# Two attention layers on one core: bias lines of a head group written in one transfer from a mirrored grid, and the normalising product moved from VectorE to GpSimd

## The chip, the cores and the metric

One Trainium2 chip, of which the kernel uses a single core. The metric is the device time in microseconds (us). The kernel before was timed three times: median 1791.99 us, lowest 1791.25, highest 1793.11. The time after comes from the same measurement.

## The reference

The input is x of shape (8, 256, 32, 32): 8 batch elements, 256 channels, 1024 positions. Two layers follow each other. The shapes of the weights are left out.

```python
# layer 0
xn = (x - mean) / jnp.sqrt(var + EPS) * gamma          # mean and variance over the channels
q, k, v = jnp.split(einsum('oc,bcn->bon', w_qkv, xn), 3, axis=1)   # 8 heads of 32
sim = einsum('bhdi,bhdj->bhij', q, k) * scale
bias = _cpb_bias(32, w0, b0, w1, b1, w2, b2)           # a small network of (yi - yj, xi - xj), per head
out = einsum('bhij,bhdj->bhdi', softmax(sim + bias), v)
x = einsum('oc,bcn->bon', w_out, out) + x
# layer 1
f, g, h = Wf x + bf, Wg x + bg, Wh x + bh              # f, g of 32 channels, h of 256
attn = softmax(einsum('bno,bom->bnm', f, g), axis=2)
return gamma * einsum('bci,bij->bcj', h, attn) + x
```

The bias depends only on the difference of two positions, so a table of 63 x 63 values for each head holds all of it.

## The kernel before, in words

The 8 heads are two groups g of HG = 4, one for each half of 256 channels. For each batch element b the kernel goes through four phases: the rows of group 0, the columns of group 0, the rows of group 1, the columns of group 1, each of 32 tiles of 128 x 1024 scores.

- In a **rows** phase (tile m) TensorE computes the scores of 128 queries against all keys (L587, L588), VectorE adds the bias and takes the maximum (L1015), and ScalarE exponentiates and sums (L829). This gives each query its shift.
- In a **columns** phase (tile n) TensorE computes scores again, transposed and with the shift folded in (L608), VectorE adds the bias (L1029), ScalarE exponentiates (L846), and TensorE multiplies by v (L635).

All engines run their programs in order and meet at semaphores. Everything else is placed beside these tiles by four tables written by hand, `side_0`, `column_0`, `side_1` and `column_1`: an entry `(3, "norm", 0)` of `column_0` stands behind tile n = 3 of the columns of group 0. In this way the normalisation and the q and k of element b+1 (kinds "mean", "centre", "square", "var", "rstd", "norm", "k0", "q0") and layer 1 of element b-1 are done beside element b. Of the normalisation, "centre" (L873) subtracts the mean on VectorE, "rstd" (L716, L712) leaves 1/std in `o[:, 1]`, and "norm" (L879) multiplies the two halves of `xn` by it, each 128 x 1024 floats, on VectorE. TensorE's "k0", first needed behind n = 14, and all later users of `xn` wait for it through the semaphore `normed`.

q and k change their layout by a trip through DRAM. They are split into a high and a low part in the buffer `st` (ScalarE writes the high part, VectorE the low one, kinds "high_..." and "low_..."), `q_out` and `k_out` (L298) write `st` to `q_parts` and `k_parts`, and `q_in` (L311, 6 transfers) and `k_in` (L325, 3 transfers) load `q_stack` and `k_stack`. `st` is one buffer for both, so the next high part waits until the transfer before it has been stored.

The bias is brought into place once, at the start. A small network on TensorE, ScalarE and VectorE computes the table, SP stores it to DRAM (L367, L368), and then for each group g and each column x = 0 ... 31 one transfer `lines_out` (L330) copies 252 runs of 32 floats (4 heads x 63 rows) from the table to `bias_lines` in DRAM: for group 0 sixteen are issued by SP and sixteen by ScalarE, for group 1 all 32 by SP. SP waits until a group is stored, and then `bias_in` (L362) loads it to `bias_lines_sb` by 16 transfers of 240 KB. Group 0's first rows tile needs the first head of group 0; group 1's rows phase needs group 1. Behind `bias_in(1)` in SP's program stand `q_out` and `q_in` of group 1 and the load of x for element 1.

ScalarE at the start: it computes 1/std, waits for the table, issues its sixteen `lines_out`, and only then does it handle `high_k0`, `k_out`, `high_q0`, `q_out`, `k_in`, `q_in` of element 0, after which the first rows tile can start.

As the stored table runs with rising difference, the keys or queries of one side are read backwards: the moving operand of L587 and L588 is `back(keys, ...)`, that of L608 is `q_stack[..., ::-1]`.

Of the kernel before, what the change touches and what calls it, by code (L numbers as in the profile page):

```python
# [25 lines left out]
def two_layer_attention(nc, x, mlp_in, rel_in, wqkv_in, gamma_in, ident_in, wout_in, wh_in, wfg_in, bfg_in,  # L26
# [23 lines left out]
    with ExitStack() as ctx:  # L50
# [82 lines left out]
        lines_stored = sem("lines_stored")  # L133
        late_lines_stored = sem("late_lines_stored")
# [27 lines left out]
        VECTOR = dict(centered=KC, normed=KC, lo_ready=2 * (NHALF + 1), a_max=G * HG * NT, scaled=G * NHALF,  # L162
# [6 lines left out]
        for kind in (TENSOR, VECTOR, SCALAR):  # L169
            for name, n in kind.items():  # L170
                counted(name, n)
# [31 lines left out]
        column_0 = [(1, "rstd", 1), (3, "norm", 0), (9, "norm", 1)]  # L203
# [69 lines left out]
        def row_tile(m):  # L273


            r, rest = divmod(m, HM)
            h, t = divmod(rest, NT // NHALF)
            return r, h, (NHALF - 1 - r) * (NT // NHALF) + t
# [49 lines left out]
        def lines_out(eng, g, x, done):  # L328
            src = table_dram.ap().rearrange("h (a w) -> h a w", w=DX)[g * HG:(g + 1) * HG, :, W - 1 - x:2 * W - 1 - x]
            eng.dma_start(lines_dram.ap()[g, x], src).then_inc(done, 16)  # L330

# [3 lines left out]
        def _(sp):  # L335
# [6 lines left out]
            def shift_to_stack(b, g, r):  # L342

                need(sp, "rows_ready", b, g * NHALF + r + 1)
                for part in range(2):
                    sp.dma_start(q_stack[KS + part:KS + part + 1, g, NHALF - 1 - r].bitcast(F32)
                                 .rearrange("p h (t n) -> p (h t) n", n=P),
                                 shift_rows[part * HM:(part + 1) * HM, r, :].bitcast(F32)).then_inc(rows_loaded, 16)
# [10 lines left out]
            def bias_in(g):  # L359
                for h in range(HG):  # L360
                    for yl in range(ROWS):
                        sp.dma_start(bias_lines[yl * W:(yl + 1) * W, g * HG + h],  # L362
                                     lines_dram.ap()[g, :, h, ROWS - 1 - yl:ROWS - 1 - yl + NA]
# [7 lines left out]
            for x in range(0, W, 2):  # L371
                lines_out(sp, 0, x, lines_stored)
            sp.wait_ge(lines_stored, 16 * W)
            bias_in(0)
            for x in range(W):
                lines_out(sp, 1, x, late_lines_stored)
            sp.wait_ge(late_lines_stored, 16 * W)
            bias_in(1)
# [30 lines left out]
        def _(pe):  # L409
# [167 lines left out]
            def row_tiles(b, g, first, m):  # L577
# [9 lines left out]
                pe.matmul(psum[:, bank, :], lhsT, back(keys, 0, HALF, N), start=True, stop=True)  # L587
                pe.matmul(psum[:, bank + 1, :], lhsT, back(keys, HALF, HALF, N), start=True,  # L588
# [8 lines left out]
            def columns_phase(b, g, first, last):  # L597


                for q in range(TG + PV_LAG):  # L600
                    if q < TG:
                        for n in range(q * HP, (q + 1) * HP):
# [4 lines left out]
                            for i in range(2):  # L607
                                mm = pe.matmul(psum[:, bank + i, :], k_stack[:, g, 2 * j + i, t * P:(t + 1) * P],  # L608
                                               q_stack[:, g, NHALF - 1 - half, 2 * j + i, ::-1],
# [81 lines left out]
        def _(act):  # L691
# [87 lines left out]
            def output(b, g, half, last):  # L779
# [83 lines left out]

        @block.vector
        def _(dve):
# [3 lines left out]
            def do(kind, arg, b, g, first, last, tail=False):  # L869
# [127 lines left out]
            for k in range(KC):  # L997
                do("norm", k, 0, 1, True, False)
# [4 lines left out]
            def element(b, first, last):  # L1003
                for g in range(G):
                    for m in range(A_TILES):
                        r, h, t = row_tile(m)
                        a0 = (H - ROWS - ROWS * t) * W
# [12 lines left out]
                    for n in range(SN):  # L1020
                        half, t, j = column_tile(n)
                        a0 = (half * (H // NHALF) - ROWS * t + H - ROWS) * W
# [35 lines left out]
def relative_grid(side):  # L1058

    d = np.arange(1 - side, side, dtype=np.float32)  # L1060
# [61 lines left out]
```

## Time and profile before

| | before |
|---|---|
| median of 3 runs | 1791.99 us |
| the profiled execution, its own time | 1792.51 us |
| its span, first to last instruction | 1790.7 us |
| TensorE, busy | 1590.5 us (89%) |
| VectorE, busy | 1478.0 us (83%) |
| ScalarE, busy | 1382.0 us (77%) |
| GpSimd, busy | 7.1 us |
| DMA moved | 122.71 MB, 58121 packets, 22292 of them under 512 B |
| mean granted TensorE clock | 0.936 |

The span is what the trace covers, the execution's own time has 1.8 us around it. Busy time of TensorE is not time at its peak, since its matmuls overlap, and a mean over the span hides stages: the page's row of 40 slices shows TensorE at 6, 2 and 6 tenths in its first three slices of 44.8 us, and at 8 or 9 nearly everywhere after.

### The profile page before, as it was taken

How to read it: one execution, taken by the hardware profiler on the slowest of the kernel's cores; microseconds unless marked ns; L12 is line 12 of the kernel's file. 1: busy time of each engine (PE TensorE's matmuls, PEld its weight loads, DVE VectorE, ACT ScalarE, POOL GpSimd, SP SyncE). 2: the span in 40 equal slices, each digit the busy share in tenths (PEclk: the TensorE clock that was granted, in tenths of full speed). 3: DMA queues.
4: the chain of work that ended last, by engine and by line, in shares of the span. 5: the costliest groups of instructions: out<-in, count | busy, mean ns of one | idle time of the engine just before them, and what ended most of it. 6: DMA issues, size and time to landing. Idle time of an engine off the chain costs nothing.

```text
span 1790.7 us, 18676 instructions
## 1 busy us (share of the span) xinstructions
PE 1590.5 (89%) x5976; PEld 754.6 (42%) x5976; DVE 1478.0 (83%) x2168; ACT 1382.0 (77%) x2033; POOL 7.1 (0%) x5
## 2 busy tenths in 40 slices
PE   6268899899998999889998999989998999989988
PEld 2033334345353444435453443535444453535424
DVE  3157988898988988898888989898888989899853
ACT  2066889778887878878787888888798788889743
POOL 1000000000000000000000000000000000000000
PEclk8577869999999999999999999999999999999999
DMA  3972204320350203501152203502034102500100
GB/s 87 221 173 69 59 1 130 95 59 1 89 157 4 59 1 107 141 24 36 46 159 45 59 1 107 142 1 60 25 117 108 51 10 80 141 4 0 37 12 23
DMA packets 58121, 122.71 MB, mean 69 GB/s; under 512 B 22292, under 2 KB 23828, under 8 KB 58024
## 3 DMA queue, kind: packets, MB, share of 16 engines
q1 hardware_dynamic: 50952, 114.85, 23.3%
q10 hardware_dynamic: 7072, 6.68, 1.5%
q8 instruction: 47, 0.77, 0.2%
q14 instruction: 50, 0.41, 0.1%
HBM read 78.92 MB, written 44.13 MB: 69 GB/s over the span
## 4 chain that ended last, share of the span: by engine, by line
PE 49%; DVE 24%; issue 18%; SPq 3%; ACT 3%; DMA 2%; ACTq 1%; DVEq 0%
DVE biased L1015 13%; PE psum L533 9%; PE psum L608 9%; PE psum L635 8%; PE psum L587 5%; DVE biased L1029 5%; PE psum L413 5%; PE psum L588 4%; PE psum L456 3%; SPq L330 2%; PE psum L490 2%; PE psum L466 1%; ACT biased L829 1%; DMA xn<-in_x_dram 1%; ACT probs L846 1%
## 5 line engine op out<-in xcount | busy, mean ns | idle before, releaser
L1015 DVE CUSTOM_DVE_ANT_0 biased<-psum,bias_lines_sb 128x1024 f32<-128x1024 f32 x512 | 617.3, 1222 | 157.5 <-PE psum L588 150.1
L829 ACT ACTIVATE biased<-biased,nmax 128x1024 f32<-128x1024 f32 x512 | 587.2, 1147 | 140.5 <-DVE nmax L1015 136.1
L846 ACT ACTIVATE probs<-biased 128x1024 f32<-128x1024 f32 x512 | 536.5, 1056 | 127.9 <-DVE biased L1029 107.5
L1029 DVE TENSOR_TENSOR biased<-psum,bias_lines_sb 128x1024 f32<-128x1024 f32 x512 | 598.0, 1220 | 44.7 <-PE psum L608 34.2
L608 PE MATMUL psum<-q_stack,k_stack 98*128 98x512 f32 x1024 | 393.5, 492 | 39.3 <-DVE nmax L1015 16.2
L587 PE MATMUL psum<-k_stack,q_stack 96*128 96x512 f32 x512 | 330.2, 645 | 92.7 <-DVE nmax L1015 48.5
L608 PEld LDWEIGHTS psum<-q_stack,k_stack 98*128 98x128 f32 x1024 | 179.0, 201 | 328.2 <-issue 152.5
L635 PE MATMUL psum<-probs,vT 128*32 128x512 f32 x2048 | 283.5, 623 | 6.1 <-DVE st L896 3.9
L587 PEld LDWEIGHTS psum<-k_stack,q_stack 96*128 96x128 f32 x512 | 99.9, 195 | 277.1 <-DVE nmax L1015 176.4
L588 PE MATMUL psum<-k_stack,q_stack 96*128 96x512 f32 x512 | 211.8, 414 | 0.0
L533 PE MATMUL psum<-probs 128*128 128x512 f32 x384 | 186.6, 592 | 0.0
L588 PEld LDWEIGHTS psum<-k_stack,q_stack 96*128 96x128 f32 x512 | 102.7, 201 | 49.9 <-issue 46.4
L456 PE MATMUL psum<-xn,wqkvT 128*128 128x512 f32 x128 | 79.8, 718 | 26.1 <-DVE st L896 7.8
L829 ACT ACTIVATION_READ_ACCUMULATOR biased<-biased,nmax 128x1 f32 x512 | 96.2, 188 | 0.0
L533 PEld LDWEIGHTS psum<-probs 128*128 128x128 f32 x384 | 72.6, 189 | 46.4 <-issue 36.1
L635 PEld LDWEIGHTS psum<-probs,vT 128*32 128x32 f32 x2048 | 42.5, 109 | 101.2 <-issue 74.3
L767 ACT ACTIVATE probs<-probs,nmax 128x1024 f32<-128x1024 f32 x48 | 54.9, 1144 | 16.3 <-DVE probs L953 15.6
L413 PE MATMUL psum<-xn,wqkvT 128*128 128x512 f32 x128 | 66.4, 600 | 0.0
L466 PE MATMUL psum<-wqkvT,xn 128*128 128x256 f32 x256 | 65.7, 378 | 0.0
L502 PE MATMUL psum<-whT,x 128*128 128x256 f32 x256 | 65.5, 380 | 0.0
L478 PE MATMUL psum<-o,woutT 128*128 128x512 f32 x128 | 64.4, 593 | 0.8 <-ACT o L788 0.8
L533 PE MATMUL psum<-o,probs 128*128 128x512 f32 x128 | 64.8, 592 | 0.0
(78 smaller groups left out, 1091.0 us busy)
## 6 DMA issues: line engine op xcount, KB each, us to landing
q_stack<-q_parts SPq DMA_DIRECT2D x90, 256.0 KB, 5.5
k_stack<-k_parts SPq DMA_DIRECT2D x45, 512.0 KB, 7.4
q_parts<-st SPq DMA_DIRECT2D x15, 1024.0 KB, 3.9
k_parts<-st SPq DMA_DIRECT2D x15, 1024.0 KB, 4.2
xn<-in_x_dram SPq DMA_DIRECT2D x8, 1024.0 KB, 8.9
x<-in_x_dram SPq DMA_DIRECT2D x8, 1024.0 KB, 9.5
out_dram<-x SPq DMA_DIRECT2D x8, 1024.0 KB, 4.1
bias_lines_sb<-bias_lines SPq DMA_DIRECT2D x32, 240.0 KB, 8.0
```

The lines of the kernel that those rows point to most:

```text
L413: mm = pe.matmul(psum[0:rows, bank + half, :], lhsT(k), src[:, k, half * HALF:(half + 1) * HALF], start=(k == 0), stop=(k == KC - 1))
L456: mm = pe.matmul(psum[:, bank, :], wqkvT[:, k, t * C:t * C + P], xn[:, k, half * HALF:(half + 1) * HALF], start=(k == 0), stop=(k == KC - 1))
L466: mm = pe.matmul(psum[:, 4 + arg % 2, 0:C], xn[:, k, arg * P:(arg + 1) * P], wqkvT[:, k, 2 * C:3 * C], start=(k == 0), stop=(k == KC - 1))
L533: mm = pe.matmul(psum[:, 4 + 2 * c + half, :], hs[:, t % HS, c * P:(c + 1) * P], attn1[t % 3][:, half * HALF:(half + 1) * HALF], start=(t ...
L587: pe.matmul(psum[:, bank, :], lhsT, back(keys, 0, HALF, N), start=True, stop=True)
L588: pe.matmul(psum[:, bank + 1, :], lhsT, back(keys, HALF, HALF, N), start=True, stop=True).then_inc(SEMS["a_mm"], 1)
L608: mm = pe.matmul(psum[:, bank + i, :], k_stack[:, g, 2 * j + i, t * P:(t + 1) * P], q_stack[:, g, NHALF - 1 - half, 2 * j + i, ::-1], star ...
L635: mm = pe.matmul(psum[h * HD:(h + 1) * HD, 4 + half, :], vT[:, t, (g * HG + h) * HD:(g * HG + h + 1) * HD], probs[:, ((q - PV_LAG) * HP + ...
L829: nc.scalar.activation(biased[:, m % BIASED, :], biased[:, m % BIASED, :], ACT.Exp, scale=-1.0, bias=nmax[:, m:m + 1], accum_out=rowsum[:, ...
L846: nc.scalar.activation(probs[:, n % P_SLOTS], biased[:, n % BIASED, :] .rearrange("p (i n) -> p i n", i=2), ACT.Exp).then_inc(SEMS["probs_ ...
L1015: nc.vector.tensor_tensor_reduce(biased[:, m % BIASED, :], pair(bank_of(g, first, ("rows", m))), bias_lines[:, g * HG + h, a0:a0 + N], -1. ...
L1029: nc.vector.tensor_tensor(biased[:, n % BIASED, :].rearrange("p (i n) -> p i n", i=2), psum[:, bank:bank + 2, :], bias_lines[:, g * HG + 2 ...
```

## The change

There are two edits that are independent of each other.

**The lines.** The grid of differences is built with falling instead of rising differences (`np.arange(side - 1, -side, -1)`), so the table is mirrored in both directions. The line of column x now starts at x in each table row, and the 32 columns of a group are one access pattern of overlapping runs: 32 x 252 x 32 floats with steps 1, 63, 1. Each group is one transfer, both are issued by SP, one behind the other and each with its own semaphore. ScalarE issues none. The two `bias_in` follow behind both. The rest follows the mirror: where a tile's bias starts (`a0`), the order of the two halves of the queries, keys and queries read forwards, and the output `o` written backwards.

**The product.** "norm" goes out of VectorE's program and out of `column_0`. GpSimd multiplies both halves of `xn` by 1/std, as soon as "centre" and "rstd" are done.

```diff
-        column_0 = [(1, "rstd", 1), (3, "norm", 0), (9, "norm", 1)]
+        column_0 = [(1, "rstd", 1)]
...
-            for x in range(0, W, 2):
-                lines_out(sp, 0, x, lines_stored)
-            sp.wait_ge(lines_stored, 16 * W)
-            bias_in(0)
-            for x in range(W):
-                lines_out(sp, 1, x, late_lines_stored)
-            sp.wait_ge(late_lines_stored, 16 * W)
-            bias_in(1)
+            for g in range(G):
+                src = bass.AP(tensor=table_dram.ap().tensor, offset=g * HG * DY * DX,
+                              ap=[[1, W], [DX, HG * DY], [1, W]])
+                sp.dma_start(lines_dram.ap()[g].rearrange("x h a w -> x (h a) w"), src).then_inc(lines_stored[g], 16)
+            for g in range(G):
+                sp.wait_ge(lines_stored[g], 16)
+                bias_in(g)
...
-                pe.matmul(psum[:, bank, :], lhsT, back(keys, 0, HALF, N), start=True, stop=True)
-                pe.matmul(psum[:, bank + 1, :], lhsT, back(keys, HALF, HALF, N), start=True,
+                pe.matmul(psum[:, bank, :], lhsT, keys[:, 0:HALF], start=True, stop=True)
+                pe.matmul(psum[:, bank + 1, :], lhsT, keys[:, HALF:N], start=True,
...
-                                               q_stack[:, g, NHALF - 1 - half, 2 * j + i, ::-1],
+                                               q_stack[:, g, half, 2 * j + i, :],
...
-                nc.scalar.copy(o[:, g, half * HALF:(half + 1) * HALF],
-                               psum[:, 4 + half, :]).then_inc(SEMS["o_ready"], 1)
+                nc.scalar.copy(back(o[:, g, :], half * HALF, HALF, N), psum[:, 4 + half, :]).then_inc(SEMS["o_ready"], 1)
...
-            act.wait_ge(table_stored, 32)
-            for x in range(1, W, 2):
-                lines_out(nc.scalar, 0, x, lines_stored)
...
+            def normalise(b, k):
+                need(pool, "centered", b, KC)
+                need(pool, "rstd_ready", b, 2)
+                nc.gpsimd.tensor_tensor(xn[:, k, :], xn[:, k, :], rstd, ALU.mult).then_inc(SEMS["normed"], 1)
+
+            for b in range(B):
+                for k in range(KC):
+                    normalise(b, k)
...
-                elif kind == "norm":
-                    if arg == 0:
-                        need(dve, "rstd_ready", b, 2)
-                        need(dve, "centered", b, KC)
-                    nc.vector.tensor_tensor(xn[:, arg, :], xn[:, arg, :], rstd, ALU.mult).then_inc(SEMS["normed"], 1)
...
-    d = np.arange(1 - side, side, dtype=np.float32)
+    d = np.arange(side - 1, -side, -1, dtype=np.float32)
```

SP's program at the start, before: `bias_table` is the stored table, `bias_lines` the lines in DRAM, `bias_lines_sb` those in SBUF.

```order
L367 DMA bias_table<-probs 8x2016 [waits table_ready]
L368 DMA bias_table<-probs 8x1953
L330 DMA bias_lines<-bias_table 252x32 [waits table_stored]
L330 DMA bias_lines<-bias_table 252x32 x15
L362 DMA bias_lines_sb<-bias_lines 32x1920 [waits lines_stored]
L362 DMA bias_lines_sb<-bias_lines 32x1920 x15
L330 DMA bias_lines<-bias_table 252x32 x32
L362 DMA bias_lines_sb<-bias_lines 32x1920 [waits late_lines_stored]
L362 DMA bias_lines_sb<-bias_lines 32x1920 x15
L298 DMA q_parts<-st 128x2x1024 [waits q_loaded,lo_ready]
```

The same stretch of SP's program now.

```order
L363 DMA bias_table<-probs 8x2016 [waits table_ready]
L364 DMA bias_table<-probs 8x1953
L370 DMA bias_lines<-bias_table 8064x1x32 [waits table_stored]
L370 DMA bias_lines<-bias_table 8064x1x32
L358 DMA bias_lines_sb<-bias_lines 32x1920 [waits lines_stored_0]
L358 DMA bias_lines_sb<-bias_lines 32x1920 x15
L358 DMA bias_lines_sb<-bias_lines 32x1920 [waits lines_stored_1]
L358 DMA bias_lines_sb<-bias_lines 32x1920 x15
L298 DMA q_parts<-st 128x2x1024 [waits q_loaded,lo_ready]
```

48 transfers of SP became two, and the 32 loads of the bias now stand behind each other with nothing but a semaphore between them.

VectorE's program in the columns phase of group 0, element 0, before: L1029 adds the bias to a tile, L923 to L935 are the shift.

```order
L1029 TENSOR_TENSOR biased<-psum,bias_lines_sb 128x1024 x4
L879 TENSOR_TENSOR xn<-xn,o 128x1024
L1029 TENSOR_TENSOR biased<-psum,bias_lines_sb 128x1024
L923 TENSOR_TENSOR invsum<-rowsum,invsum 128x16
L926 SCALAR_TENSOR_TENSOR lnsum<-invsum,lnsum 128x16
L929 TENSOR_TENSOR shift<-nmax,lnsum 128x16
L932 CAST shift_hi<-shift 128x16
L934 COPY shift_parts<-shift_hi 128x16
L935 TENSOR_TENSOR shift_parts<-shift,shift_hi 128x16
L1029 TENSOR_TENSOR biased<-psum,bias_lines_sb 128x1024 x5
L879 TENSOR_TENSOR xn<-xn,o 128x1024
L1029 TENSOR_TENSOR biased<-psum,bias_lines_sb 128x1024 x10
```

The same place now (the lines have other numbers: L1024 adds the bias, L920 to L932 are the shift).

```order
L1024 TENSOR_TENSOR biased<-psum,bias_lines_sb 128x1024 x5
L920 TENSOR_TENSOR invsum<-rowsum,invsum 128x16
L923 SCALAR_TENSOR_TENSOR lnsum<-invsum,lnsum 128x16
L926 TENSOR_TENSOR shift<-nmax,lnsum 128x16
L929 CAST shift_hi<-shift 128x16
L931 COPY shift_parts<-shift_hi 128x16
L932 TENSOR_TENSOR shift_parts<-shift,shift_hi 128x16
L1024 TENSOR_TENSOR biased<-psum,bias_lines_sb 128x1024 x15
```

The two products are gone from between the tiles. They are now 16 instructions on GpSimd, `xn<-xn,o 128x1024`, behind its fill of `k_stack`.

## Rows read from the trace of the kernel before

**Rows 1.** Timeline, the start: start us, us, engine, line, operation [idle before, releaser].
```profile
30.40 2.36 DVE L879 TENSOR_TENSOR xn<-xn,o 128x1024 f32<-128x1024 f32 x2 [0.56 <-ACT o L712]
32.73 7.84 SPq L330 DMA_DIRECT2D bias_lines<-bias_table  x10
32.91 6.54 PE L456 MATMUL psum<-xn,wqkvT 128*128 128x512 f32 x8 [3.83 <-DVE xn L879]
...
45.70 1.08 ACT L732 ACTIVATE st<-psum 128x512 fp32r<-128x512 f32 x2 [15.33 <-issue]
47.62 9.45 SPq L362 DMA_DIRECT2D bias_lines_sb<-bias_lines  x16
54.36 0.60 ACT L728 ACTIVATE st<-psum 128x512 fp32r<-128x512 f32 x1 [7.57 <-DMA k_parts<-st]
57.12 43.93 SPq L330 DMA_DIRECT2D bias_lines<-bias_table  x32
60.82 0.38 ACTq L298 DMA_DIRECT2D q_parts<-st  x1
86.38 0.77 PE L587 MATMUL psum<-k_stack,q_stack 96*128 96x512 f32 x1 [26.95 <-DMA q_stack<-q_parts]
102.76 7.81 SPq L362 DMA_DIRECT2D bias_lines_sb<-bias_lines  x16
102.95 1.22 DVE L882 SCALAR_TENSOR_TENSOR st<-psum,st 128x1024 fp32r<-128x1024 f32 x1
```

**Rows 2.** Windows: busy us of each engine, granted clock, DMA share, GB/s.
```profile
54.00:57.00 3.00, 1.17 (x2) 0.69 (x3) 0.69 (x1) 0.60 (x1) 0.00 (x0) 0.50 1.04 223
81.00:84.00 3.00, 0.00 (x0) 0.00 (x0) 0.00 (x0) 0.00 (x0) 0.00 (x0) 0.50 1.11 229
93.00:96.00 3.00, 3.00 (x12) 2.13 (x11) 1.23 (x2) 1.60 (x4) 0.00 (x0) 0.95 0.32 41
```

**Rows 3.** The chain that ended last, stretch 32 to 137 us: start us, us, what.
```profile
60.24 7.06 SPq L330
...
93.56 0.73 SPq L330
94.33 0.73 SPq L330
...
110.70 13.61 DMA q_parts<-st
127.11 9.13 DMA xn<-in_x_dram
136.29 2.07 PE psum L413 x2
```

**Rows 4.** DMA issues: engine, count, KB each, median us to landing.
```profile
q_parts<-st SPq DMA_DIRECT2D x15, 1024.0 KB, 3.9
bias_lines_sb<-bias_lines SPq DMA_DIRECT2D x32, 240.0 KB, 8.0
```

**Rows 5.** The chain around the first product, element 3's columns, group 0.
```profile
763.03 0.06 DVE xn L879
764.16 1.22 DVE biased L1029
```

**Rows 6.** The chain around the second product, elements 3 and 0.
```profile
174.94 1.00 issue
175.94 1.23 DVE biased L1029
...
773.16 0.67 PE psum L608 x2
773.83 0.86 PE psum L490 x2
```

**Rows 7.** Timeline: GpSimd's fill, and element 3's first use of the product.
```profile
0.73 6.92 POOL L862 MEMSET k_stack<- 2x8192 f32 x1 [0.29 <-POOLq L1109]
...
780.09 1.10 PE L456 MATMUL psum<-xn,wqkvT 128*128 128x512 f32 x2 [1.14 <-issue]
```

More of the change, by code:

```diff
@@ L132, in two_layer_attention @@
         table_stored = sem("table_stored")
-        lines_stored = sem("lines_stored")
-        late_lines_stored = sem("late_lines_stored")
+        lines_stored = [sem(f"lines_stored_{g}") for g in range(G)]
         consts_set = sem("consts_set")
@@ L161, in two_layer_attention @@
                       pv_mm=G * TG, proj_mm=KC * NHALF, fg_mm=3, h_mm=NT, s1_mm=NT, sa_mm=NT)
-        VECTOR = dict(centered=KC, normed=KC, lo_ready=2 * (NHALF + 1), a_max=G * HG * NT, scaled=G * NHALF,
+        POOL = dict(normed=KC)
+        VECTOR = dict(centered=KC, lo_ready=2 * (NHALF + 1), a_max=G * HG * NT, scaled=G * NHALF,
                       shifted=2 * G * NHALF, split_hi=G * NHALF,
@@ L168, in two_layer_attention @@
                       rows_ready=G * NHALF, probs_ready=G * TG * HP, o_ready=G * NHALF, fg_hi=3, e1_ready=NT, hs_ready=NT)
-        for kind in (TENSOR, VECTOR, SCALAR):
+        for kind in (TENSOR, VECTOR, SCALAR, POOL):
             for name, n in kind.items():
@@ L277, in row_tile @@
             h, t = divmod(rest, NT // NHALF)
-            return r, h, (NHALF - 1 - r) * (NT // NHALF) + t
+            return r, h, r * (NT // NHALF) + t
         def column_tile(n):
@@ L326, in k_in @@
                              k_dram.ap()[part].rearrange("h d n -> d h n")).then_inc(k_loaded, 16)
-        def lines_out(eng, g, x, done):
-            src = table_dram.ap().rearrange("h (a w) -> h a w", w=DX)[g * HG:(g + 1) * HG, :, W - 1 - x:2 * W - 1 - x]
-            eng.dma_start(lines_dram.ap()[g, x], src).then_inc(done, 16)
         block = ctx.enter_context(nc.Block())
@@ L345, in shift_to_stack @@
                 for part in range(2):
-                    sp.dma_start(q_stack[KS + part:KS + part + 1, g, NHALF - 1 - r].bitcast(F32)
+                    sp.dma_start(q_stack[KS + part:KS + part + 1, g, r].bitcast(F32)
                                  .rearrange("p h (t n) -> p (h t) n", n=P),
@@ L362, in bias_in @@
                         sp.dma_start(bias_lines[yl * W:(yl + 1) * W, g * HG + h],
-                                     lines_dram.ap()[g, :, h, ROWS - 1 - yl:ROWS - 1 - yl + NA]
+                                     lines_dram.ap()[g, :, h, yl:yl + NA]
                                      .rearrange("x a w -> x (a w)")).then_inc(lines_loaded[g * HG + h], 16)
@@ L862, in _ @@
             nc.gpsimd.memset(k_stack[KS:KS + 2].bitcast(F32), 1.0).then_inc(ones_set, 1)
+            pool.wait_ge(ones_set, 1)
+            def normalise(b, k):
[5 more added lines that the diff above has]
+                    normalise(b, k)
         @block.vector
@@ L996, in _ @@
                     do("centre", 0, 0, 1, True, False)
-            for k in range(KC):
-                do("norm", k, 0, 1, True, False)
             dve.wait_ge(consts_loaded, 16 * N_CONSTS)
@@ L1006, in element @@
                         r, h, t = row_tile(m)
-                        a0 = (H - ROWS - ROWS * t) * W
+                        a0 = ROWS * t * W
                         free = (("sum_ready", b, g * A_TILES + m - BIASED + 1) if m >= BIASED else
@@ L1021, in element @@
                         half, t, j = column_tile(n)
-                        a0 = (half * (H // NHALF) - ROWS * t + H - ROWS) * W
+                        a0 = (half * (H // NHALF) + ROWS * t) * W
                         need(dve, "s_mm", b, g * SN + n + 1)
```

## The prediction

> **What bounds the kernel now.** I read the timeline of the start first, because half of the change is there. The reader is to see three things in it [rows 1]. TensorE does not begin the first rows tile before 86.38 us, and waits 26.95 us for the load of `q_stack`. ScalarE could take the first half of k0 from TensorE soon after 36 us, but is at its own sixteen lines transfers and starts at 45.70. And the first VectorE instruction of element 0 that is not a rows tile, the low part of q, comes at 102.95, sixteen us after the first tile.
>
> Then the windows, for what the 16 DMA engines do meanwhile [rows 2]. Their share is 1.04 in 54 to 57 us, where the bias of group 0 is loaded at 223 GB/s, and 1.11 in 81 to 84: from about 48.5 to 86.3 us the transfers themselves set the time. In 93 to 96 the share is 0.32: there SP issues the lines of group 1 one by one, and the engines are mostly idle.
>
> The chain of waits shows that the start does not end at 86 us [rows 3]. SP gets to `q_out` of group 1 only at 110.70, since the sixteen loads of the bias stand before it; the store takes 13.61 us, and has 3.9 in the median of the later ones [rows 4]. The load of x follows (127.11, 9.13 us), and TensorE takes up the "mean" of element 1 at 136.29. From there on the engines set the pace, not the DMA.
>
> In the columns phases of group 0 the chain goes alternately over VectorE and TensorE. The first product lies on it: 763.03 to 764.16 is the product, and the next tile waits behind it [rows 5]. When VectorE reaches the second product of element 3, the chain is on TensorE (773.16, 773.83); in element 0, which has no layer 1 beside it, the second one is on the chain too (174.94, 1.00 us) [rows 6].
>
> **The product, part by part.** Sixteen instructions leave VectorE. Two are at the start and are treated below. Of the 14 others, the first of each of 7 elements is on the chain with 764.16 - 763.03 = 1.13 us [rows 5], 7 x 1.13 = 7.9. In element 0 the second adds 1.0, in the six others I take 0 (below: 0; above: 1.1 each, 6.6 in all, if VectorE were behind there; I take the end that the chain shows). TensorE has to be able to follow: it has waits for VectorE at this place that are about as long as the product, so I let all of it count. Together -8.9 us.
>
> On GpSimd the trace shows no such product. From below: the fill of 8192 floats a partition takes 6.92 us [rows 7], so 1024 floats cost 0.86 us for the writing alone; from above three such passes, two read and one written, 2.6 us. I take 2.6, for what reads as well as writes is nearer to it. Two of them end 5.2 us after 1/std. That is ready at about 763, and "k0" is first issued at 780.09 [rows 7], so 12 us cover it. If the cover were gone, it would cost what the products exceed 17 us by.
>
> What GpSimd does beside VectorE might slow VectorE. The trace has no pair of the two at work together on large tiles, so this price is open: none from below, and from above VectorE standing still for the 5.2 us of each of 7 elements, 36 us. I take 0, as the tiles of VectorE in this stretch read one operand from PSUM and one from SBUF.
>
> A rule of the Trainium skill bears on that (GPSIMD Engine Reference, sections 3.1 and 8): GpSimd needs 4497 ns for a product of 2048 floats a partition, about twice VectorE, and shares its SBUF interface with VectorE, which collides when the VectorE instruction has two SBUF inputs. By its figure one product here would be an estimated 2.2 us. By its condition the bias additions would not collide, and the six small instructions of the shift would. No row here shows either.
>
> **The lines.** What goes: the 64 single transfers, sixteen of them on ScalarE. What comes: two of SP, one behind the other. Work for the engines: 32 transfers of a group take, at the pace of SP, 94.33 - 93.56 = 0.77 us each [rows 3], at a share of 0.32 [rows 2], which makes 0.25 us of all sixteen engines; 64 of them are 15.7 us. Bounds for both groups together: 12 us from below, if fuller queues let the small packets follow each other more closely, and 49 us from above (64 x 0.77), if one queue cannot run faster than SP's single transfers did. I take 15.7, because that pace is SP's issue time, and the engines stood idle for two thirds of it.
>
> They begin at about 35 (table stored 32.7, 2.3 us until data moves) and end at about 50.7. Beside them the start of element 0 goes on: products on GpSimd end at 30.3 + 5.2 = 35.5 instead of 32.8, TensorE is 2.7 us later, and ScalarE takes k0 as it comes, so `k_out` is issued at about 43 instead of 47.7. But its data queue behind two large transfers of SP. I let them land when the lines are done, near 54, as before (54.36 [rows 1]). The 2.7 us of GpSimd and the 9 us of freed ScalarE are both hidden by that.
>
> Now the loads. Before, `q_stack` landed at 86.3 after 37.8 us of full engines, which carried the bias of group 0, both stores and both loads, and about 1.3 us of lines of group 1: 36.5 without them. Now SP issues the 16 loads of group 1 right behind those of group 0 (a group takes SP 9.45 us [rows 1]), so that they are in the queue before `q_out` is issued (60.82 before, about 59.5 now). They are 16 x 240 KB = 3.93 MB, at 229 GB/s [rows 2] 17.2 us. So the first tile starts at 50.7 + 36.5 + 17.2 = 104.4 instead of 86.4: +18.0.
>
> What this buys: behind the start there is no load of the bias any more. `q_out` of group 1 is issued when its low part is done, 102.95 + 1.22 = 104.2 on the old clock instead of 110.7 (-6.5), and lands in 3.9 us instead of 13.61 (-9.7) [rows 1, 3, 4]. Together -16.2. The load of x keeps its 9 us, as it still runs beside `q_in`. So "mean" of element 1 starts at 136.3 + 18.0 - 16.2 = 138.1, +1.8 us. A transfer that was to come early has only changed its place in a full queue.
>
> The Trainium skill says (DMA: Bandwidth & Descriptors, Rules for kernel authors) that many small transfers should be made one large one. Taken alone it would have the start of the tiles move forward by about the 9 us that ScalarE and SP save; by the windows above the queue is full right afterwards, and the saving does not reach the tiles.
>
> Reading and writing forwards or backwards I take as equal: the number of elements is the same, and no row shows both directions of one of these operations. That is an assumption, and the matmuls in the middle would show it.
>
> **Sum.** 1792.5 (the profiled execution) - 8.9 + 1.8 = 1785.4. The median of the runs is 0.5 lower, so 1785.
>
> **The rivals.**
> - *The transfers of q and k go first* (0.2). If the DMA engines serve ScalarE's queue in turn with or ahead of the long bias loads, only few of group 1's 17.2 us lie ahead of the first tile. It starts near 87, and the rest of the bias, then x, follow beside the tiles: "mean" near 122. That is -14 at the start, 1769 in all. For it: k0's store, issued beside the bias loads, was quick. Against it: q's store, issued at 60.82, took until 71.67.
> - *One queue is slow* (0.14). This is the other side. If the two large transfers move at the pace of SP's single ones, both need up to 49 us; each us above 15.7 delays the first tile by one, since ScalarE's k0 and the bias wait behind. From 15.7 + 7.1 + 3.6 = 26 us on the kernel is slower by more than 0.2%; at 36 us, halfway to the bound, it is 1785 + 20 = 1805. Against it: the share of 0.32.
> - *GpSimd slows VectorE, or TensorE does not follow* (0.2). Then the 8.9 us are lost in part or wholly; with 1.8 at the start, 1787 to 1794, with heavy collisions above 1800.
>
> **How the numbers follow.** My forecast has 0.46, with its own range 1780 to 1790. What a measurement can tell from no change is 0.2%, 3.6 us, so faster is below 1788.4 and slower above 1795.6. Faster: 0.36 of the forecast, 0.2 of the first rival, 0.03 of the third. Same: 0.1 of the forecast, 0.02 of the second, 0.1 of the third. Slower: 0.12 of the second and 0.07 of the third. The range 1767 to 1802 reaches to the first rival and some way into the second.
>
> **What would show it.** In the profile after: the two lines transfers end near 51 us; the share of the DMA engines is near 1 from there to the first tile, near 104; `q_parts` of group 1 lands in about 4 us; "mean" of element 1 starts near 138; the products take 2 to 2.6 us on GpSimd and the bias additions on VectorE keep 1.22. The forecast is wrong if the first tile starts before 95 or after 115, if the additions beside a product are longer, or if the length of an element in the middle does not fall by about 1.1 us.

## The result

The changed kernel takes 1802.78 us in the median (1801.11 to 1804.38, four runs), the kernel before 1792.55 beside it. The ratio is 1.0056 with a 95% interval of 1.0041 to 1.007: slower by 10 us, where 1785 was forecast. The time lies just outside the range. The two edits went in opposite directions: the start became shorter, where it was forecast 1.8 us longer, and each element that has a product beside its columns became longer.

| | before | after |
|---|---|---|
| profiled execution: span | 1790.7 us | 1799.3 us |
| TensorE / VectorE / ScalarE busy | 1590.5 / 1478.0 / 1382.0 us | 1588.5 / 1482.5 / 1382.2 us |
| GpSimd busy | 7.1 us | 44.6 us |
| mean granted TensorE clock | 0.936 | 0.934 |
| first rows tile starts | 86.38 us | 95.73 us |
| "mean" of element 1 starts | 136.29 us | 131.03 us |

VectorE has sixteen instructions less, 19.4 us of work, and is busy for 4.5 us more. That is the first thing to notice. The groups of instructions by line say where it went (busy us, mean ns of one, then idle time before them). First two rows of the shift before:

```profile
L926 DVE SCALAR_TENSOR_TENSOR lnsum<-invsum,lnsum 128x16 f32<-128x16 f32 x32 | 5.6, 174 | 1.1
L923 DVE TENSOR_TENSOR invsum<-rowsum,invsum 128x16 f32<-128x16 f32 x32 | 5.4, 170 | 0.0
```

The same after, with the product and the bias additions:

```profile
L1024 DVE TENSOR_TENSOR biased<-psum,bias_lines_sb 128x1024 f32<-128x1024 f32 x512 | 597.5, 1216 | 53.3 <-PE psum L603 39.8 <-ACT biased L820 7.7 <-ACT probs L837 2.9
L860 POOL TENSOR_TENSOR xn<-xn,o 128x1024 f32<-128x1024 f32 x16 | 37.5, 2366 | 1349.2 <-ACT o L707 1349.2
L923 DVE SCALAR_TENSOR_TENSOR lnsum<-invsum,lnsum 128x16 f32<-128x16 f32 x32 | 20.2, 632 | 1.1
L920 DVE TENSOR_TENSOR invsum<-rowsum,invsum 128x16 f32<-128x16 f32 x32 | 13.1, 409 | 0.0
```

Two instructions on 16 floats a partition cost 22.3 us more (20.2 - 5.6 + 13.1 - 5.4), while the 512 large additions have kept their 1.22 us. The timeline of element 3, at the place of [rows 5], shows the moment:

```profile
765.04 4.70 POOL L860 TENSOR_TENSOR xn<-xn,o 128x1024 f32<-128x1024 f32 x2 [203.61 <-ACT o L707]
...
766.17 1.30 DVE L920 TENSOR_TENSOR invsum<-rowsum,invsum 128x16 f32<-128x16 f32 x1
...
767.51 2.26 DVE L923 SCALAR_TENSOR_TENSOR lnsum<-invsum,lnsum 128x16 f32<-128x16 f32 x1
769.80 0.17 DVE L926 TENSOR_TENSOR shift<-nmax,lnsum 128x16 f32<-128x16 f32 x1
...
770.62 0.61 PE L567 MATMUL psum<-ident,shift_parts 128*32 128x128 f32 x2 [3.37 <-DVE shift_parts L932]
...
771.66 1.22 PE L603 MATMUL psum<-q_stack,k_stack 98*128 98x512 f32 x2 [0.43 <-DVE biased L1024]
...
772.82 1.93 PE L630 MATMUL psum<-probs,vT 128*32 128x512 f32 x8
```

GpSimd's two products run from 765.04 to 769.74. L920 starts inside the first and ends (767.47) when the first product, 2.35 us long, is over. L923 starts inside the second and ends (769.77) when that is over. Behind the two TensorE is idle for 3.37 us, and then its matmuls take nearly twice their time (eight L630 1.93 us instead of 1.06). The windows (length; busy us of PE, its weight load, DVE, ACT, POOL; then granted clock, DMA share, GB/s) show the clock granted there, 0.50, which is the lower of the two levels, 1.2 GHz, behind a stretch in which TensorE was nearly idle:

```profile
764.00:767.00 3.00, 3.00 (x16) 1.04 (x14) 3.00 (x3) 3.00 (x4) 1.96 (x1) 1.00 0.00 0
767.00:770.00 3.00, 0.26 (x2) 0.00 (x0) 2.91 (x3) 0.75 (x1) 2.74 (x2) 1.00 0.00 0
770.00:773.00 3.00, 1.94 (x8) 0.87 (x12) 2.77 (x6) 1.36 (x2) 0.00 (x0) 0.50 0.00 0
...
776.00:780.00 4.00, 4.00 (x17) 1.49 (x15) 2.96 (x3) 2.02 (x2) 0.00 (x0) 0.90 0.02 4
```

In the kernel before the windows from 764 to 784 us have 1.00 throughout. The chain of waits, which had `xn L879` in [rows 5], has the two held instructions in its place:

```profile
766.26 1.22 DVE invsum L920
767.51 2.27 DVE lnsum L923
```

How long an element is can be read from the "centre" instructions, of which each element has two, one behind the other. The row gives shortest/median/longest ns, and first and last start; x12 are the elements 2 to 7. Before:

```profile
L873 DVE TENSOR_TENSOR xn<-xn,psum x12: 1214/1214/1218, 328.2 to 1361.9; 128x1024 f32<-128x1024 f32 x12
```

After:

```profile
L875 DVE TENSOR_TENSOR xn<-xn,psum x12: 1214/1215/1217, 327.1 to 1370.3; 128x1024 f32<-128x1024 f32 x12
```

Less 1.1 us for the second of the pair, five elements take 1032.6 us before and 1042.1 after: 206.5 and 208.4 us each. The forecast had each of them shorter by 1.1 us.

The start after, in the timeline, for comparison with [rows 1]:

```profile
28.77 4.63 POOL L860 TENSOR_TENSOR xn<-xn,o 128x1024 f32<-128x1024 f32 x2 [21.12 <-ACT o L707]
30.97 6.42 SPq L370 DMA_DIRECT2D bias_lines<-bias_table  x2
...
39.48 18.94 SPq L358 DMA_DIRECT2D bias_lines_sb<-bias_lines  x32
41.59 0.39 ACTq L298 DMA_DIRECT2D k_parts<-st  x1
...
95.73 0.77 PE L582 MATMUL psum<-k_stack,q_stack 96*128 96x512 f32 x1 [42.24 <-DMA q_stack<-q_parts]
...
114.38 0.38 SPq L298 DMA_DIRECT2D q_parts<-st  x1
119.27 2.69 SPq L311 DMA_DIRECT2D q_stack<-q_parts  x6
131.03 2.07 PE L408 MATMUL psum<-xn,mean_w 128*128 128x512 f32 x2 [1.31 <-DMA xn<-in_x_dram]
```

The two large transfers land 8.5 and 13.8 us after their issue, as the row of their line says:

```profile
DMA to landing us min/median/max: 8.5/11.1/13.8
```

Group 0's lines are there at 39.5 and group 1's at 45.5. From there to the first tile the DMA engines are full, and behind it they are empty:

```profile
47.00:54.00 7.00, 3.59 (x4) 1.18 (x4) 0.69 (x1) 1.07 (x2) 0.00 (x0) 0.56 1.06 243
54.00:70.00 16.00, 0.00 (x0) 0.00 (x0) 0.69 (x1) 0.12 (x1) 0.00 (x0) 0.58 1.01 288
70.00:95.00 25.00, 0.00 (x0) 0.00 (x0) 0.00 (x0) 0.00 (x0) 0.00 (x0) 0.50 1.00 232
95.00:99.00 4.00, 2.68 (x6) 1.66 (x6) 1.93 (x3) 0.60 (x1) 0.00 (x0) 0.50 0.00 0
```

So the bias of group 1 lies wholly ahead of the first tile, as forecast, and the first tile is later than before by 9.3 us; but `q_parts` of group 1 is issued without sixteen loads in front of it and lands in 4.9 us, and "mean" of element 1 starts 5.3 us earlier than before.

### The profile page after: what moved, and what is told of

Read it like the earlier page. It is cut to its first block, busy times and chain, and to the rows that moved or that the text cites. A ratio compares the mean times of both kernels' runs of the same rounds, so it can differ in the third digit from the quotient of the medians.

```text
span 1799.3 us, 18624 instructions
## 1 busy us (share of the span) xinstructions
PE 1588.5 (88%) x5976; PEld 753.9 (42%) x5976; DVE 1482.5 (82%) x2152; ACT 1382.2 (77%) x2033; POOL 44.6 (2%) x21
## 4 chain that ended last, share of the span: by engine, by line
PE 50%; DVE 25%; issue 18%; ACT 3%; DMA 3%; POOL 0%; DVEq 0%; ACTq 0%; SPq 0%; POOLq 0%
DVE biased L1010 13%; PE psum L528 9%; PE psum L603 9%; PE psum L630 8%; PE psum L582 6%; PE psum L408 6%; DVE biased L1024 5%; PE psum L583 4%; PE psum L451 4%; PE psum L461 2%; PE psum L485 1%; DMA q_stack<-q_parts 1%; ACT biased L820 1%; DVE probs L938 1%; DVE lnsum L923 1%
## 5 line engine op out<-in xcount | busy, mean ns | idle before, releaser
L1024 DVE TENSOR_TENSOR biased<-psum,bias_lines_sb 128x1024 f32<-128x1024 f32 x512 | 597.5, 1216 | 53.3 <-PE psum L603 39.8
L603 PE MATMUL psum<-q_stack,k_stack 98*128 98x512 f32 x1024 | 395.0, 492 | 37.6 <-DVE nmax L1010 16.2
L582 PE MATMUL psum<-k_stack,q_stack 96*128 96x512 f32 x512 | 330.3, 645 | 98.0 <-DMA q_stack<-q_parts 42.2
L603 PEld LDWEIGHTS psum<-q_stack,k_stack 98*128 98x128 f32 x1024 | 179.6, 201 | 328.8 <-DVE biased L1024 157.0
L630 PE MATMUL psum<-probs,vT 128*32 128x512 f32 x2048 | 284.3, 625 | 6.2 <-DVE st L893 4.0
L582 PEld LDWEIGHTS psum<-k_stack,q_stack 96*128 96x128 f32 x512 | 100.0, 195 | 282.8 <-DVE nmax L1010 166.4
L583 PE MATMUL psum<-k_stack,q_stack 96*128 96x512 f32 x512 | 210.1, 410 | 0.0
L583 PEld LDWEIGHTS psum<-k_stack,q_stack 96*128 96x128 f32 x512 | 102.7, 201 | 50.1 <-issue 46.7
L451 PE MATMUL psum<-xn,wqkvT 128*128 128x512 f32 x128 | 75.7, 685 | 25.0 <-DVE st L887 8.0
L630 PEld LDWEIGHTS psum<-probs,vT 128*32 128x32 f32 x2048 | 42.6, 109 | 102.4 <-issue 74.3
L860 POOL TENSOR_TENSOR xn<-xn,o 128x1024 f32<-128x1024 f32 x16 | 37.5, 2366 | 1349.2 <-ACT o L707 1349.2
L408 PE MATMUL psum<-xn,wqkvT 128*128 128x512 f32 x128 | 66.9, 604 | 0.0
```

The costliest lines, as they stand in the source:

```text
L408: mm = pe.matmul(psum[0:rows, bank + half, :], lhsT(k), src[:, k, half * HALF:(half + 1) * HALF], start=(k == 0), stop=(k == KC - 1))
L451: mm = pe.matmul(psum[:, bank, :], wqkvT[:, k, t * C:t * C + P], xn[:, k, half * HALF:(half + 1) * HALF], start=(k == 0), stop=(k == KC - 1))
L582: pe.matmul(psum[:, bank, :], lhsT, keys[:, 0:HALF], start=True, stop=True)
L583: pe.matmul(psum[:, bank + 1, :], lhsT, keys[:, HALF:N], start=True, stop=True).then_inc(SEMS["a_mm"], 1)
L630: mm = pe.matmul(psum[h * HD:(h + 1) * HD, 4 + half, :], vT[:, t, (g * HG + h) * HD:(g * HG + h + 1) * HD], probs[:, ((q - PV_LAG) * HP + ...
L1024: nc.vector.tensor_tensor(biased[:, n % BIASED, :].rearrange("p (i n) -> p i n", i=2), psum[:, bank:bank + 2, :], bias_lines[:, g * HG + 2 ...
```

## The experiments

The theory from these rows: VectorE's small shift instructions stand still while a GpSimd product runs (theory "held"; the expectations call it T), and this costs all that is lost. The rivals: the lines edit loses the time in the start or through the reading direction; the product is late for TensorE's "k0"; the stall comes from the semaphore waits around the shift.

### One edit at a time

`e1_product_only` is the kernel before with only the product moved, `e2_lines_only` the changed kernel with the product back between VectorE's tiles.

```diff
-        column_0 = [(1, "rstd", 1)]
+        column_0 = [(1, "rstd", 1), (3, "norm", 0), (9, "norm", 1)]
```

> The kernel before with the product alone moved to GpSimd; the lines stay as they were. Theory T (the shift's small VectorE instructions, which read two SBUF operands, stand still until GpSimd's product has ended; the lines edit by itself is a gain): the elements in the middle are as long as in the kernel after, the start as in the kernel before; the loss is 8.6 (what the kernel after lost in its span) + 5.6 (what it gained until the centring of element 1), some 14 us: 1806, ratio 1.008. Rival R (the lines edit is what costs, the product is neutral or a gain of 8.9): 1783 to 1793.

> The kernel after with the product back on VectorE. T: the elements in the middle as before, the start 5 to 7 us shorter: 1786, ratio 0.997. R: 1800 or above.

Measured: the product alone 1809.8 us, ratio 1.0088 (1.0075 to 1.0102); the lines alone 1785.89, ratio 0.9961 (0.9947 to 0.9975). By the ratios that is +15.8 and -7.0 us, together +8.8 of the +10 measured for both, so the two edits add up within their intervals. The product alone loses more than the 14 us expected of it, and the lines are not what loses the time. In e1 the timeline of element 3 has the same pair of held instructions:

```profile
772.10 4.68 POOL L870 TENSOR_TENSOR xn<-xn,o 128x1024 f32<-128x1024 f32 x2 [204.50 <-ACT o L713]
773.23 1.29 DVE L930 TENSOR_TENSOR invsum<-rowsum,invsum 128x16 f32<-128x16 f32 x1
...
774.56 2.26 DVE L933 SCALAR_TENSOR_TENSOR lnsum<-invsum,lnsum 128x16 f32<-128x16 f32 x1
```

### The same work without the meeting

`e3_shift_later` is the changed kernel with the shift put behind four more tiles, where the products are over:

```diff
-        column_0 += [(4, "shift", 1), (6, "turn", 1), (6, "keep_rows", 1)]
+        column_0 += [(8, "shift", 1), (10, "turn", 1), (10, "keep_rows", 1)]
```

> The kernel after with the shift of the second half behind tile 8 instead of 4 of the columns (turn and keep_rows behind 10 instead of 6), so that GpSimd's 4.7 us are over when it comes. T: L920 and L923 take 0.17 us again, TensorE's clock does not fall there, and what the kernel after lost comes back together with the 8.9 us that I predicted for the product: 1779, ratio 0.993. Rival C (GpSimd's work slows VectorE's large additions too, or the product's leaving VectorE buys nothing since TensorE does not follow): 1786 to 1800.

`e7_product_after_shift` leaves VectorE's order as it is and has GpSimd wait until the shift of the element in work is done:

```diff
                 need(pool, "rstd_ready", b, 2)
+                need(pool, "parts_ready", b - 1, NHALF)
```

> The kernel after, with VectorE's order untouched, and GpSimd waiting in addition until the last instruction of the shift (parts_ready) is done. T: L920 and L923 take 0.17, the product starts some 2.5 us later and still ends before k0 is issued; the time is that of the kernel with the shift later, 1774 to 1780. If it was the place of the shift and not the overlap with GpSimd that cost, this kernel stays near 1802. What the low part of g (L910, one SBUF and one PSUM input) does beside the product is seen too: 0.74 us if only VectorE instructions without PSUM collide.

Measured: e3 1776.16 us, ratio 0.9905 (0.9891 to 0.9919); e7 1777.76, ratio 0.9919 (0.9905 to 0.9932). Either way of keeping the two apart gives back some 25 us, against the loss of 22.3 us in VectorE's two rows. As e7 leaves the shift where it was in VectorE's order, the place of the shift is not what cost. It answers the last question of its expectation too: the low part of g (L911), with one operand in PSUM and one in SBUF, ran beside a product and kept its 0.74 us:

```profile
753.59 4.73 POOL L861 TENSOR_TENSOR xn<-xn,o 128x1024 f32<-128x1024 f32 x2 [199.97 <-DVE shift_parts L933]
```
```profile
756.85 0.74 DVE L911 SCALAR_TENSOR_TENSOR fg_stack<-psum,bfg,fg_stack 32x512 fp32r<-32x512 f32 x1
```

In e3 the shift is what it was, and "centre" gives 204.5 us an element (1347.5 - 1.1 - 324.0 over five):

```profile
L923 DVE SCALAR_TENSOR_TENSOR lnsum<-invsum,lnsum 128x16 f32<-128x16 f32 x32 | 5.6, 175 | 1.1
L920 DVE TENSOR_TENSOR invsum<-rowsum,invsum 128x16 f32<-128x16 f32 x32 | 5.4, 168 | 0.0
```
```profile
L875 DVE TENSOR_TENSOR xn<-xn,psum x12: 1214/1214/1217, 324.0 to 1347.5; 128x1024 f32<-128x1024 f32 x12
```

Some 0.4 to 0.6 us an element are lost beyond VectorE's 22.3 us. I put them down to TensorE's idle stretch and the half clock behind it. That is argued from the windows and not shown: it is a difference of runs, and no run isolates the clock.

### What VectorE waits for

If it waits for the end of the running GpSimd instruction, shorter instructions must make shorter waits. `e4_product_in_eight` is the changed kernel with each product in eight pieces:

```diff
-                nc.gpsimd.tensor_tensor(xn[:, k, :], xn[:, k, :], rstd, ALU.mult).then_inc(SEMS["normed"], 1)
+                for part in range(8):
+                    cols = slice(part * P, (part + 1) * P)
+                    mul = nc.gpsimd.tensor_tensor(xn[:, k, cols], xn[:, k, cols], rstd[:, cols], ALU.mult)
+                mul.then_inc(SEMS["normed"], 1)
```

> The kernel after with each product cut into 8 instructions of 128x128. If a VectorE instruction waits until the running GpSimd instruction ends (T1), L920 and L923 wait 0.3 to 0.5 us each instead of 1.1 and 2.1, and the kernel is near 1784. If it waits until GpSimd has nothing to do (T2), or both share the port evenly (T3), the stall stays at 3 us or more: 1800 or above, as GpSimd's own time grows with 8 times the fixed cost.

Measured: 1789.42 us (1783.19 to 1791.69 in eleven runs), ratio 0.9974 (0.9963 to 0.9986), where T1 had 1784. Sixteen pieces take 6.70 us, 0.42 each, and the timeline has every instruction of the shift but the first held until about the end of a piece:

```profile
759.31 6.70 POOL L862 TENSOR_TENSOR xn<-xn,o 128x128 f32<-128x128 f32 x16 [200.04 <-ACT o L707]
```
```profile
760.44 0.20 DVE L923 TENSOR_TENSOR invsum<-rowsum,invsum 128x16 f32<-128x16 f32 x1
760.67 0.38 DVE L926 SCALAR_TENSOR_TENSOR lnsum<-invsum,lnsum 128x16 f32<-128x16 f32 x1
...
761.50 0.39 DVE L932 CAST shift_hi<-shift 128x16 fp32r<-128x16 f32 x1
761.92 0.38 DVE L934 COPY shift_parts<-shift_hi 128x16 f32<-128x16 f32 x1
762.21 0.50 DVE L935 TENSOR_TENSOR shift_parts<-shift,shift_hi 128x16 f32<-128x16 f32 x1
```

The wait scales with GpSimd's instruction, as T1 says and T2 and T3 don't. T1 had named two instructions that wait; five of the six do, for 1.2 us together, and GpSimd is at work for 6.70 us instead of 4.70. What of the 5 us too many each of these makes, no run tells. And the cast and the copy, which have one input, wait too. To tell whether that is the operand or the neighbourhood, `e8_probes_on_vector` takes e3, in which nothing meets the products, and adds three small instructions there:

```diff
+        column_0 = [(1, "rstd", 1), (4, "probe", 0), (5, "probe", 1), (6, "probe", 2)]
...
+                    nc.vector.tensor_scalar(probe[:, 0, 0:15], ident[:, 0:15], 2.0, None, ALU.mult)
+                    nc.vector.tensor_copy(probe[:, 1, :], ident[:, 16:32])
+                    nc.vector.tensor_tensor(probe[:, 2, :], ident[:, 32:48], ident[:, 48:64], ALU.add)
```

> The changed kernel with the shift at n = 8 and turn and keep_rows at n = 10, and three small VectorE instructions of 15 or 16 floats a partition added beside the products of GpSimd, each behind a tile of the columns of group 0: behind n = 4 a tensor_scalar with one SBUF input and an SBUF output, behind n = 5 a copy SBUF to SBUF, behind n = 6 a tensor_tensor of two SBUF inputs. The output is the reference's. Theory A (a VectorE instruction waits for the running GpSimd instruction to end whenever it has no operand in PSUM): each of the three that meets a running product lasts up to 2.3 us, the three that fall behind it 0.05 to 0.2 us; the products last 4.7 us, so at most three tiles see them. Theory B (only two SBUF inputs are held): the tensor_scalar and the copy last under 0.2 us although a product runs beside them, the tensor_tensor up to 2.3 us. Theory C (it is the semaphore waits of the shift, not its operands): none of the three is longer than 0.2 us. Time of the kernel: 1777 to 1786 us by A (up to 2 x 1.2 us in each of seven elements), 1776 to 1781 by B and C.

Measured: 1801.12 us in one run. The products of element 3 run from 764.05 to 768.80:

```profile
765.37 1.11 DVE L879 TENSOR_SCALAR probe<-ident 128x15 f32<-128x15 f32 x1
766.40 1.21 DVE L1031 TENSOR_TENSOR biased<-psum,bias_lines_sb 128x1024 f32<-128x1024 f32 x1
767.53 1.30 DVE L881 COPY probe<-ident 128x16 f32<-128x16 f32 x1
...
769.88 0.16 DVE L883 TENSOR_TENSOR probe<-ident 128x16 f32<-128x16 f32 x1
```

The tensor_scalar ends at 766.48 and the copy at 768.83, at the ends of the first and the second product; the tensor_tensor came after both, so this run says nothing of it (e1 and the changed kernel do, by L930 and L920). None of the three has a wait, and the bias additions in between, with one operand in PSUM, run at full speed beside GpSimd. So it is the operands: one input and an output in SBUF are enough. The kernel's time missed all three expectations: 25 us over e3 for 2.1 us of holding in each of seven elements, 15 us in all. TensorE's timeline shows where the rest may lie, an idle of the same kind as in the changed kernel, with a granted clock of 0.56 from 773 to 776 us. Its next step there needs the low part of g (L917), which VectorE does only behind the probes:

```profile
772.00 1.10 PE L486 MATMUL psum<-x,wfgT 128*96 128x512 f32 x2 [3.29 <-DVE fg_stack L917]
...
773.56 1.94 PE L631 MATMUL psum<-probs,vT 128*32 128x512 f32 x8
```

### The start

`e6_before_bias1_late` is the kernel before with `bias_in(1)` moved behind the first shift rows of element 0, past `q_out`, `q_in` and the load of x:

```diff
-            sp.wait_ge(late_lines_stored, 16 * W)
-            bias_in(1)
...
                     shift_to_stack(b, 0, r)
+                    if first and r == 0:
+                        sp.wait_ge(late_lines_stored, 16 * W)
+                        bias_in(1)
```

> The kernel before, with the sixteen loads of group 1 behind the first shift rows of element 0 and nothing else changed. By my step (q_out of group 1 issued at 104.2 instead of 110.7 and landing in 3.9 instead of 13.6) the mean of element 1 starts 16 us earlier: 1776, ratio 0.991. If the load of x or k_in then becomes the last, less: 1780 to 1785.

Measured: 1776.92 us, ratio 0.9915 (0.9902 to 0.9929), 15 us less than before, where 1776 was expected. Its `q_out` of group 1 goes out at 105.38 instead of 110.70, and is followed 3.9 us later by the loads:

```profile
105.38 0.39 SPq L298 DMA_DIRECT2D q_parts<-st  x1
109.30 2.96 SPq L311 DMA_DIRECT2D q_stack<-q_parts  x6
```

`e9_bias1_late` does the same to e3; `e5_group1_late` also moves the lines transfer of group 1, behind the load of x:

```diff
-            for g in range(G):
-                sp.wait_ge(lines_stored[g], 16)
-                bias_in(g)
+            lines_out(0)
+            sp.wait_ge(lines_stored[0], 16)
+            bias_in(0)
...
                     sp.dma_start(xn[:], x_dram[b + 1]).then_inc(x_loaded, 16)
+                if first:
+                    lines_out(1)
...
                     shift_to_stack(b, 0, r)
+                    if first and r == 0:
+                        sp.wait_ge(lines_stored[1], 16)
+                        bias_in(1)
```

> As the run before, but the second lines transfer stays behind the first; only the sixteen loads of group 1 are late. D: the second lines transfer costs 5 to 7 us, since the store of k queues behind it (41.59 to 48.4 in the kernel after), so some 5 us slower than the run before: 1768. If the large lines transfers were harmless to ScalarE's queue, the two runs are equal within 1.

> The kernel with the shift later (e3), and of group 1 the lines transfer moved behind the load of x for element 1 and the sixteen loads of the bias behind the first shift rows of element 0. Theory D (group 1's 17.2 us of bias loads run in turns with the q and k transfers of element 0 and delay the first tile, and nobody needs them before 200 us): q_stack lands before 82, the first tile starts by 82 instead of 96 to 97, the mean of element 1 by 118 instead of 131; 1776 - 13 = 1763. Rival S (the first tile is set by the layout trips of q and k, or the late loads delay the load of x or the k of group 1 in their turn): a gain under 4, 1772 to 1776.

Measured: e9 1761.46 us, ratio 0.9827 (0.9813 to 0.984); e5 1758.41, ratio 0.9807 (0.9794 to 0.982). Both came out below their expectations (1768 and 1763), and the lines transfer of group 1, which was to cost 5 us ahead of the first tile, is worth 3. e5 is the fastest kernel of the study, 34 us under the kernel before. In e9 the first tile starts at 82.08, 13.6 us before that of the changed kernel: that is what the bias of group 1 had cost in front of it. In e5 it is at 78.78.

`e10_vector_product_group1_late` is e5 with the product back on VectorE and the shift at its old place, to weigh the product alone in the best arrangement:

```diff
-        column_0 = [(1, "rstd", 1)]
-        column_0 += [(8, "shift", 1), (10, "turn", 1), (10, "keep_rows", 1)]
+        column_0 = [(1, "rstd", 1), (3, "norm", 0), (9, "norm", 1)]
+        column_0 += [(4, "shift", 1), (6, "turn", 1), (6, "keep_rows", 1)]
```

> The best arrangement so far (lines of group 1 behind the load of x, its bias behind the first shift rows of element 0) with the product back on VectorE between the tiles, and the shift back at n = 4, turn and keep_rows at n = 6. If the product is worth one VectorE instruction of 1.13 us on the chain of each element and 1.0 more in element 0, as the prediction had it, this run takes 1758.4 + 8.9 = 1767 us (ratio to the kernel before 0.986); if both products of an element are on the chain, 1758.4 + 15.8 = 1774. If the start, and not the product, hides part of it (rival), 1758 to 1763. Mean length of an element in the middle: 205.9 to 206.5 us by the first, 204.9 by the last.

Measured: 1768.01 us (1764.64 to 1769.32), ratio 0.9868 (0.9851 to 0.9884), 9.6 us over e5. From e2 to e3, the same pair with the old start, it is 9.7. Both pairs also move the shift; e7, which doesn't, is 8.1 us under e2. Of the start e10 shows the other side: with VectorE's faster product its first tile is at 75.57, 3.2 us before that of e5.

## Why the prediction was wrong

Point by point, by its own steps.

- **VectorE's slowdown by GpSimd, taken as 0 (bounds 0 and 36 us): this is the step that failed.** It costs 22.3 us of VectorE's time and about 26 us in all (1802.78 against e3's 1776.16; by the ratios to the kernel before 1.0056 and 0.9905). The reason given for 0 was that VectorE's tiles read one operand from PSUM. That is true of the tiles, which did keep 1.22 us, and beside the point: the order of VectorE's program, which the text showed, has the six shift instructions of 0.17 us right behind the next tile, inside the 5 us of the products. The bound of 36 us came from the right picture, standing still for 5.2 us; the shift stood still for 3.2. As a sum over the seven elements that is 7 x (1.13 + 2.1) = 22.6. Their short length hid them; an operation that is held until another ends costs what is left of the other, not a share of its own time. The rule of the Trainium skill that the prediction quoted (GPSIMD Engine Reference, sections 3.1 and 8) named these six and was given no price. Its page "SBUF — State Buffer" (section "SBUF: two separate sides") has the size as well: the shared ports are an exclusive lock, whichever instruction starts first has them to its end, and the other blocks fully. The traces here agree: 1.30 and 2.26 us beside a product of 2.35, 0.38 beside pieces of 0.42. With it the sum of the prediction would have come out near 1808 (1785.4 + 22.6), as an estimate.
- **The product's worth, -8.9 us: right in sum.** 9.7 (e2 to e3), 9.6 (e10 to e5) and 8.1 (e2 to e7). Its split is less sure: an element in the middle gained 1.4 us from e2 to e3 and to e7, and 0.9 from e10 to e5, where 1.1 was forecast.
- **The product on GpSimd, 2.6 us (bounds 0.86 and 2.6): 2.35**, and its cover of 12 us before "k0" held; TensorE waits for it only at the start.
- **The lines, 15.7 us of work from 35 to 50.7: it was 14.5 us from the issue at 30.97 to the landing at 45.5**, and the first group was there after 8.5. The issue at 30.97 is itself 1.8 us earlier than the 32.73 of before. The rival of the slow queue is out. `k_parts`, which was to land near 54 behind the lines, had landed by 48.44, when ScalarE took up q, so the lines did not hold it as long as was thought.
- **The bias of group 1 wholly in front of the first tile: right, but less dear.** The first tile starts at 95.73, not at 104.4. Of the 8.7 us, 5.2 are the earlier end of the lines, and 3.5 are the loads: 50.2 us from 45.5 to the first tile where 53.7 were counted. This split is one of bookkeeping: group 0's loads were issued from 39.48 on, beside the second lines transfer, which the sum had put one behind the other. The 17.2 us for 3.93 MB was worked out at 229 GB/s, the rate of a window of three microseconds; over 47 to 95 us it is 252 GB/s ((7 x 243 + 16 x 288 + 25 x 232) / 48), where stores are under way as well. By e9 the group is worth 13.6 us in that place.
- **`q_out` of group 1 and the load of x come earlier, -16.2 us: right.** e6, which has only this, gains 15 us. In the changed kernel the transfer takes 4.9 us (3.9 forecast).
- **The start in sum, +1.8 us: it was -5.3 at "mean" of element 1 (-6.9 in e2, 129.44 against 136.29) and -7.0 for the kernel (e2).** At "mean" the miss is 7.1 us, and the mis-sized term above, 8.7 us, covers it. That e2's two figures agree is in part luck: its first "centre" of element 2 is only 4.0 us earlier (324.2 against 328.2), and the rest comes from elements in the middle that are 0.6 us shorter, which the last section leaves open.
- **Forwards and backwards alike: right** for the matmuls: L582 645 ns, L583 410, L603 492 in the mean, as before within 4 ns, and the copy to `o` that now writes backwards takes 566 ns as before. Whether the shorter elements of e2 have to do with the direction is open.
- **The middle element, -1.1 us: it was +1.9**, from the held shift; without it (e3, and e7 with 204.5 us an element) it is -2.0.

The sum, in the terms that the runs give: -9.7 for the product, -7.0 for the start, +26 for the held shift and TensorE behind it make +9.3, where +10.2 was measured. These three are steps from one kernel to the next (before, e2, e3, after) and add up by construction. What tests them is e1: there -9.7 and +26 should give some +16, and +15.8 was measured. That the time lies less than 1 us outside the range is luck: the start was forecast 8.8 us too long, which hid a third of the 26. The third rival ("heavy collisions above 1800") is what happened, at a chance of 0.2 and with most of that put on light ones.

## What to carry to other kernels

Before work goes to GpSimd, list by VectorE's program order every instruction that will run in that stretch and has all its operands in SBUF, the tiny ones first: each that starts while GpSimd works costs the rest of GpSimd's instruction. Move them out of the stretch, or let GpSimd start behind them; splitting its work only shortens each wait and multiplies their number (1789 us against 1776). A transfer that is not yet needed should be issued behind the ones that are, however idle its queue is: moved by a few lines, group 1's bias gave 15 us, more than either edit of the change.

## What the runs showed of the hardware

- A VectorE instruction on SBUF alone (tensor_tensor, scalar_tensor_tensor, cast, copy, tensor_scalar) waits for the running GpSimd tensor_tensor to end: 1.30 and 2.26 us instead of 0.17 beside products of 2.35, and 0.38 beside pieces of 0.42. Instructions with one operand in PSUM don't (1.21 us for the addition in e8, 0.74 for L911 in e7). The sections that the prediction quoted ask for two SBUF inputs or a two-port mode, of which it gave only the first, and their 4497 ns is for an addition. Advanced Engine Details and Errata of the Trainium skill (section "2x-2p Requirements") lists source and destination in SBUF with an even, or an odd and equal, number of elements as what such a mode needs, beside its being enabled; the probes of 16 and of 15 floats both meet that and were both held, so the runs agree with it.
- In the profile the waiting instruction counts as busy, and nothing names GpSimd as the one waited for. Only its length, 1.30 us where it has 0.17 elsewhere, gives it away.
- One transfer of 8064 runs of 128 bytes landed after 8.5 us, where group 0's 32 single ones of 252 runs had taken 14.9 us, from 32.73 to the load behind them at 47.62 [rows 1].
- Still open: where both halves are read forwards, an element in the middle is about 0.5 us shorter with the same product on VectorE (e2 and e10 205.9 and 206.0 us, the kernel before and e6 206.5), with equal means of the matmuls. No run looked for the reason.
